# An attention and feed-forward block in two phases on one core: one item of each kind per group of heads, and the layernorms' normalisations moved from ScalarE to VectorE

## What is computed

```python
x = L0_attn_hidden_states                        # 16 x 512 x 512, float32
x = x + _layernorm(attention(_layernorm(x)))     # 32 heads of 16 channels, causal
x = x + _layernorm(ffn(_layernorm(x)))           # 512 -> 1408 -> 512, silu(g) * u
...
q, k, v = split_heads(x @ Wq.T + bq), split_heads(x @ Wk.T + bk), split_heads(x @ Wv.T + bv)
q, k = apply_rope(apply_rope(q, freqs_abs), freqs_temp), apply_rope(apply_rope(k, freqs_abs), freqs_temp)
scores = where(causal, q @ k.T / sqrt(16), -inf)
out = softmax(scores) @ v
return out @ Wo.T + bo
```

## Time and profile before

| what | value |
|---|---|
| median of 3 runs | 2912.18 us (2911.25 to 2916.76) |
| the profiled execution, its own time | 2921.86 us |
| its span, first to last instruction | 2920.1 us |
| mean granted TensorE clock | 0.967 of full speed |
| busy share of the span: PE, DVE, ACT, POOL | 87%, 74%, 48%, 35% |
| attention phase | the start to about 1900 us, 16 sequences |
| feed-forward phase | from about 1900 us to the end |

### The profile page before, as it was taken

The page is one execution under the profiler, slowest core; times in us unless marked ns, Lnnn a source line. Parts: engine busy times, 40 slices in busy tenths (PEclk is TensorE's granted clock), DMA queues, the critical chain, the costliest instruction groups (busy, mean ns, idle before and its releaser), DMA issues. The chain is left out here.

```text
span 2920.1 us, 56573 instructions
## 1 busy us (share of the span) xinstructions
PE 2550.0 (87%) x19584; PEld 1224.1 (42%) x19584; DVE 2174.2 (74%) x6399; ACT 1408.2 (48%) x1838; POOL 1024.1 (35%) x1083
## 2 busy tenths in 40 slices
PE   4888888888888888888888888519999999999997
PEld 1344443443443443443444444204444444444443
DVE  5898998998898888989889888264545554555554
ACT  2566666666666666666666666342222222222221
POOL 4456465465365465564564663200000000000000
PEclk8999999999999999999999999759999999999999
DMA  4232332332332332332322322130111111111111
GB/s 166 78 86 82 93 111 78 104 106 72 115 106 67 106 108 78 108 100 77 108 89 86 114 68 78 47 163 15 72 43 57 43 66 48 53 48 58 57 43 44
DMA packets 125299, 236.54 MB, mean 81 GB/s; under 512 B 11440, under 2 KB 94896, under 8 KB 111920
## 3 DMA queue, kind: packets, MB, share of 16 engines
q1 hardware_dynamic: 123056, 232.84, 25.3%
q10 hardware_dynamic: 2048, 1.05, 0.1%
HBM read 148.39 MB, written 84.41 MB: 80 GB/s over the span
## 5 line engine op out<-in xcount | busy, mean ns | idle before, releaser
L710 DVE CUSTOM_DVE_ANT_0 mx<-mx,causal 128x512 f32<-128x512 f32 (+3 forms) x2048 | 944.2, 519 | 90.0 <-PE mx L831 89.7
L550 ACT ACTIVATE probs<-ts,exp_scale 128x1024 f32<-128x1024 f32 x640 | 711.6, 1112 | 523.4 <-PE ts L845 454.4
L459 POOL TENSOR_SCALAR_AFFINE_SELECT probs<-probs 128x512 f32<-128x512 f32 x512 | 323.3, 648 | 623.1 <-ACT probs L550 623.1
L1255 DVE SCALAR_TENSOR_TENSOR hidden<-gu,up_scale,silu 128x512 f32<-128x512 f32 x176 | 132.0, 750 | 418.1 <-PE gu L1305 418.1
L1114 ACT ACTIVATE silu<-gu,gate_scale 128x512 f32<-128x512 f32 x176 | 120.9, 687 | 631.8 <-PE gu L1305 631.8
L1089 POOL TENSOR_TENSOR f_rstd<-f_var,f_neg_half 128x4 f32<-128x4 f32 x32 | 32.3, 1009 | 929.2 <-DVE f_var L1232 647.3
L1303 PE MATMUL gu<-f_xT_hi,gate_hi 128*128 128x512 f16 x704 | 267.9, 381 | 52.1 <-issue 52.1
L859 PE MATMUL xb<-probs,vs 128*32 128x512 f32 (+3 forms) x4096 | 311.9, 446 | 1.3 <-POOL probs L459 1.0
L710 DVE DVE_READ_ACCUMULATOR2_ANT row_max<- 128x1 f32 x2048 | 288.8, 141 | 0.0
L817 PE MATMUL xb<-xT_hi,w_hi 128*128 128x512 f16 x512 | 204.1, 399 | 85.6 <-DVE aT_lo L681 59.1
L845 PE MATMUL ts<-qT,kT 64*128 64x512 f16 (+3 forms) x2048 | 247.6, 300 | 34.9 <-ACT probs L550 34.7
(11 more groups left out here) (148 smaller groups left out, 4588.9 us busy)
## 6 DMA issues: line engine op xcount, KB each, us to landing
slots<-half SPq DMA_DIRECT2D x260, 128.0 KB, 12.4
qT<-slots SPq DMA_DIRECT2D x128, 256.0 KB, 3.8
kT<-slots SPq DMA_DIRECT2D x128, 256.0 KB, 4.0
xn<-x SPq DMA_DIRECT2D x16, 1024.0 KB, 5.1
xr<-x SPq DMA_DIRECT2D x16, 1024.0 KB, 5.3
slots<-half SPq DMA_DIRECT2D x256, 64.0 KB
x<-xr SPq DMA_DIRECT2D x16, 1024.0 KB, 5.7
f_xn<-x SPq DMA_DIRECT2D x16, 1024.0 KB, 4.8
```

Source lines behind the costliest of these rows:

```text
L459: nc.gpsimd.affine_select(out=d, in_=d, compare_op=ALU.is_ge, fill=0.0, base=0, pattern=[[0, HG], [1, P]], channel_multiplier=-1).then_inc ...
L550: nc.scalar.activation(probs[:, g % 2, u, :, :], ts[:, :, :], ACT.Exp, scale=exp_scale[:, 0:1]).then_inc(ts_read, 1)
L710: last = nc.vector.tensor_tensor_reduce(out=scores, in0=scores, in1=causal[:, T - P * (qt + 1):T], scale=1.0, scalar=-3e38, op0=ALU.add, o ...
```

## The change

The tables of units are replaced by a regular pattern. Each group has one q or k item (units 0 and 1), one transposed tile of x or of the attention result (unit 2), and one v or output item (units 3 and 4). The steps of a q or k item stand in the same units of every group: bias on ACT, cosine on VectorE and all of POOL's part in unit 2, high half in unit 4, low half in unit 0 of the next group, DMAs in units 1 and 2 of it. `xT_hi` and `xT_lo` become double, `aT_hi` and `aT_lo` get a fifth tile. The eight normalisations of a sequence move to VectorE, `minus_mean` and `offset` go, x is loaded, measured and turned nearly one body earlier, ACT's loop is written out, ACT's shift DMAs stand behind the exponential of unit 2, and POOL's first mask moves from unit 2 to unit 4.

```diff
-        xT_hi = sb("xT_hi", [P, NC, T], F16)
-        aT_hi = sb("aT_hi", [P, NC, T], F16)
+        xT_hi = sb("xT_hi", [P, 2, NC, T], F16)
+        aT_hi = sb("aT_hi", [P, NC + 1, T], F16)
...
-        PROJECTED = ((("q", 3, 0), ("k", 3, 0)), (("v", 3, 0), ("out", 0, -1)), (("out", 1, -1), ("out", 2, -1)),
-                     (("q", 0, 1), ("k", 0, 1)), (("out", 3, -1), ("q", 1, 1)), (("k", 1, 1), ("q", 2, 1)),
-                     (("k", 2, 1), ("v", 0, 1)), (("v", 1, 1), ("v", 2, 1)))
-        TRANSPOSED_AT = {4: ("a", 3, -1), 9: ("x", 0, 1), 10: ("x", 1, 1), 14: ("x", 2, 1), 15: ("x", 3, 1),
-                         24: ("a", 0, 0), 29: ("a", 1, 0), 39: ("a", 2, 0)}
-        STATISTICS_AT = {0: 0, 1: 1, 2: 2, 3: 3}
-        VARIANCE_AT = 4
-        NORMALISE_AT = {6: (0, 1), 7: (2,), 8: (3,)}
-        STATISTICS1_AT = {11: 0, 13: 1, 16: 2, 23: 3}
-        VARIANCE1_AT = 24
-        NORMALISE1_AT = {26: (0, 1), 27: (2,), 28: (3,)}
-        RESIDUAL_AT = {27: (0, 1), 28: (2,), 29: (3,)}
...
+        QUERIES_KEYS = [((g - 2) % NG, (g - 2) // NG + 1) for g in range(NG)]
+        V_OR_OUT = (("v", 3, 0), ("out", 0, -1), ("out", 1, -1), ("out", 2, -1), ("out", 3, -1),
+                    ("v", 0, 1), ("v", 1, 1), ("v", 2, 1))
+        TURNED = (("x", 3, 1), ("a", 3, -1), ("x", 0, 2), ("a", 0, 0), ("x", 1, 2), ("a", 1, 0), ("x", 2, 2), ("a", 2, 0))
+        STATISTICS_AT = {5: (0, 1), 6: (2, 3)}
+        VARIANCE_AT = 6
+        ROOT_AT = 8
+        NORMALISE_AT = {10: (0, 1), 11: (2, 3)}
+        STATISTICS1_AT = {11: 0, 16: 1, 21: 2, 26: 3}
+        VARIANCE1_AT = 26
+        ROOT1_AT = 28
+        NORMALISE1_AT = {30: (0, 1), 31: (2, 3)}
+        RESIDUAL_AT = {31: (0, 1), 35: (2, 3)}
...
@@ sync
-                    if s == 16 and exists(i + 1) and (not isinstance(i, int) or i + 2 < NB):
+                    if u == 1 and exists(i + owner):
+                        send_slots(i + owner, n)
+                    if u == 2 and exists(i + owner):
+                        fetch_slots(i + owner, n)
+                    if s == 3 and exists(i + 2):
                         sp.wait_ge(xT_full, NC * (i + 2))
                         sp.dma_start(xn[:, :, :], x[i + 2, :, :, :]).then_inc(x_in, 16)
-                    if s == 31 and exists(i - 1):
+                    if s == 38 and exists(i - 1):
                         sp.wait_ge(x1_ready, NT * i)
                         sp.dma_start(x1[i - 1, :, :, :], xr[:, :, :]).then_inc(x1_out, 16)
-                    if s == 33 and exists(i - 1) and exists(i):
+                    if s == 39 and exists(i - 1) and exists(i):
...
@@ scalar
-            def normalise_x(i, t):
-                if t == 0:
-                    act.wait_ge(offset_ready, i + 1)
-                nc.scalar.activation(xn[:, t, :], xn[:, t, :], ACT.Identity, bias=offset[:, t:t + 1],
-                                     scale=rstd[:, t:t + 1]).then_inc(xn_ready, 1)
...
+                    if u == 2:
+                        if exists(i + owner):
+                            add_bias(i + owner, n)
+                        if exists(i + (g + 1) // NG):
+                            read_shift(i + (g + 1) // NG, (g + 1) % NG)
+                    if u == 3:
+                        kind, c, of = TURNED[g]
+                        if in_turn(kind, i + of):
+                            (high_of_x if kind == "x" else high_of_attention)(i + of, c, bank_of(kind, c))
+                        if exists(i + (g - 1) // NG):
+                            read_weighed(i + (g - 1) // NG, (g - 1) % NG)
                     if exists(i):
                         exponential(i, g, u)
+                    if u == 2 and exists(i + (g + 1) // NG):
                         place_shift(i + (g + 1) // NG, (g + 1) % NG)
...
@@ vector
-                nc.vector.tensor_scalar(minus_mean[:, :], mv[:, :, 0], -1.0, None, ALU.mult)
...
+            def normalise_x(i, t):
+                if t == 0:
+                    dve.wait_ge(rstd_ready, i + 1)
+                nc.vector.tensor_scalar(xn[:, t, :], xn[:, t, :], mv[:, t, 0:1], rstd[:, t:t + 1],
+                                        ALU.subtract, ALU.mult).then_inc(xn_ready, 1)
+
+            def normalise_projected(i, t):
+                if t == 0:
+                    dve.wait_ge(rstd1_ready, i + 1)
+                nc.vector.tensor_scalar(y[:, t, :], y[:, t, :], mv1[:, t, 0:1], rstd1[:, t:t + 1],
+                                        ALU.subtract, ALU.mult).then_inc(projected_normed, 1)
...
@@ tensor
+                    n, owner = QUERIES_KEYS[g]
+                    if u < 2 and exists(i + owner):
+                        project_queries_keys(i, n, owner, u)
...
+                    if u == 2:
+                        kind, c, owner = TURNED[g]
+                        if in_turn(kind, i + owner):
+                            wait_for_bank(pe, i, kind, c)
+                            (turn_x if kind == "x" else turn_attention)(i + owner, c, bank_of(kind, c))
...
+                    if u >= 3:
+                        kind, n, owner = V_OR_OUT[g]
+                        if exists(i + owner):
+                            (project_v if kind == "v" else project_out)(i, n, owner, u - 3)
```

## The result

The changed kernel takes 2930.22 us (median of 20 runs, 2922.33 to 2936.29) against 2914.05 us before (20 runs): a ratio of 1.0051, 95% interval 1.0041 to 1.006. It is slower by half a per cent, where 1.8% less was forecast. The profiled execution has a span of 2928.9 us, against 2920.1 before.

What follows compares the result with a forecast made beforehand. VectorE and PE, neither full, hold each other up. 101.6 + 1.8 + 3.2 + 1.4 + 0.7 + 0.3 = 109.0 us a sequence against 112.8, so 53 us off: 2859 us, range 2824 to 2894 (8 in 10: 2800 to 2930).

Steps and rivals of the forecast that it cites:

- the late load of x: In group 1, x lands late and VectorE waits 1.5 us: +1.8 us a sequence, bounds 0 to +5.
- the statistics of x: In group 1, four statistics and the variance take 3.0 us on VectorE, of which up to 1.9 are free.
- group 6: Four normalisations with no transposition waiting, POOL's residual ahead of its products: +0.7 us a sequence, bounds 0 to 3.
- The mechanism of the old order: Work comes in lumps that stop one engine, then starve the other; PE waits 6.6 us a sequence for low halves.
- The term of 12.7 us for a regular group: On PE, 11.95 us of pure work, 0.65 for `oT` and 0.1 for the bank; eight groups make 101.6.
- the 0.65 us for `oT`: In a regular group PE waits 0.65 us for `oT`, as ScalarE's shift DMAs ahead of it take 1.4 us.
- Group 2, +3.2 and +1.4 us: PE's transposition waits for x's normalisations, +3.2 us (bounds +1.5 to +6); PE's clock then drops, +1.4 (0 to 2).
- Both ends of the attention phase stay: At the attention phase's ends nothing changes: as many q and k items lie before the first scores as before.
- x comes far too late: Rival: SP's queue delays x to 7.6 us into group 1; 114.2 us a sequence, 2932 us, chance 0.10.
- the port decides: Rival: each of eight normalisations waits for a whole POOL instruction; 114.0 us a sequence, 2929 us, chance 0.12.
- the two signs: The forecast is wrong if regular groups take over 13.2 us, or VectorE waits over 4 us for x.

Runs made afterwards that it cites:

- e1: The changed kernel with the load of x moved ahead of the fetch in SyncE's queue: 2870.24 us, ratio 0.9851 to the kernel before.
- e13: e1 with the projected rows' normalisations moved to units 30 and 35, residuals to 31 and 36: 2806.5 us, ratio 0.9636.
- e9: The changed kernel with the early load, normalisations moved to units 9, 10, 30 and 35, residuals to 31 and 36: 2767.34 us, ratio 0.9504.
- e3: The changed kernel with the early load of x and the eight normalisations back on ScalarE: 2794.77 us, ratio 0.9593.
- e6: The kernel before with ScalarE's loop over bodies 1 to 13 written out, nothing else: 2905.88 us, ratio 0.998.
- e10: e3 with the four statistics of x spread over units 5, 6, 7, 8 and the variance in 8: 2772.34 us, ratio 0.9533.
- e11: The changed kernel with the late load kept and only the places of normalisations and residuals changed as in e9: 2826.13 us, ratio 0.9712.
- e4: The kernel before with the eight normalisations on VectorE in the same units, nothing else moved: 2912.24 us, ratio 0.9998.

## Why the prediction was wrong, step by step

Three terms of the sum failed: the late load of x (1.8 us a sequence, measured 4.7), the statistics of x (nearly nothing, measured up to 3.4) and group 6 (0.7, measured 4.7). The bullets take them in turn.

Mean times, from the starts of `weigh`, over twelve whole sequences of each run. Groups 1 and 2 are the time from group 1's `weigh` to group 3's, group 6 from its `weigh` to group 7's; all in us:

| run | groups 1 and 2 | group 6 | sequence |
|---|---|---|---|
| changed kernel | 36.8 | 17.0 | 115.4 |
| e1, early load | 32.1 | 16.8 | 110.4 |
| e13, and the projected rows' places | 31.1 | 12.7 | 105.8 |
| e9, and x's places | 28.0 | 12.7 | 102.7 |
| regular groups | 24.6 | 12.3 | |

- **The mechanism of the old order was right.** PE's waits for low halves in regular groups are gone, and the regular order alone (e3) is worth 119 us against the kernel before (some 5 of them may be ScalarE's loop, e6). It was even undersized. One reading of it was wrong: the 6.6 us a sequence were the row of the weight loads (PEld), and the matmuls' own idle time for `aT_lo` in that view was 37.0 us in 8 sequences, 4.6 each:

```profile
PE xb L817 <- DVE aT_lo L681: 37.0, 32, 2.7
```

  The term of 12.7 us for a regular group measured 12.2 to 12.3: the 0.65 us for `oT` didn't come, because ScalarE issues its shift DMAs while the exponential runs.

```profile
1008.09 1.09 ACT L464 ACTIVATE probs<-ts,exp_scale 128x1024 f32<-128x1024 f32 x1
1008.21 1.20 ACTq L476 DMA_DIRECT2D qT<-shift_rows  x2
1009.46 0.60 ACT L443 ACTIVATE aT_hi<-xb 128x512 f16<-128x512 f32 x1 [0.28 <-issue]
```

  I had put the DMAs behind the exponential, 1.4 us later (the earlier trace rows shows them where nothing covers them).
- **Group 1, +1.8 us for the late x, was mis-sized.** Taking the load forward gave 59 to 60 us, 4.2 a sequence (4.7 in groups 1 and 2 of the table), and the wait is 4.3 to 4.5 us instead of 1.5. The parts: x lands after 7.1 us, not 5.5; x1 is written 1.3 us later in group 7 of the body shown than I put it; the groups between are 0.4 us shorter each, so VectorE is there sooner; and the way from that write to the load's issue is 0.8 us shorter (14.6 us, 988.86 to 1003.45, for 15.4). The longer landing comes in a place where a fetch of `kT` has just been issued and the next sends follow; before, SyncE issued nothing for some 10 us ahead of the load and 16 behind it (load at 683.26 us). That this is its reason is likely and not shown. The range "0 to +5" held the term; the value chosen was at the wrong end.
- **Group 1's statistics, put at nearly nothing, cost something too.** I let 1.9 of their 3.0 us vanish in VectorE's idle time. But with x early and no normalisation held (e9), groups 1 and 2 still take 3.4 us more than two regular ones. In the body shown above, PE waits there for the low half that stands behind the statistics on VectorE:

```profile
1025.27 0.39 PE L750 MATMUL xb<-w_hi,aT_hi 128*128 128x512 f16 x1 [2.76 <-DVE aT_lo L601]
```

  No row had this term. e10 shows that the lump is part of it; how much of the 3.4 us it makes stays open.
- **Group 2, +3.2 and +1.4 us, was right in kind.** The pair in unit 11 is held, PE waits 3.04 us for it where I had 3.6, and the clock drops as in the earlier trace rows. The x half of the edit in e9 gave 39 us, 2.8 a sequence, or 3.1 by the table: less than the 4.6 of the sum.
- **Group 6, +0.7 us, is the step whose reasoning failed.** I let VectorE take the port between POOL's instructions at little loss, and argued that no transposition waits for these rows. But all that stands behind them on VectorE is late: the cosine (itself held), then the low half `xT_lo`, for which PE stops for 3.02 us and falls to the lower clock (0.51 granted from 1091 to 1093 us). The group takes 4.7 us more than a regular one, above the bound of 3, and e13 puts 64 us, 4.6 a sequence, on these rows' places.
- **Summed**, 8 x 12.3 + (22.8 + 13.9 - 24.6) + 4.7 is 115.2, where I had 101.6 + 7.4. The bounds I gave (0 to 5, 1.5 to 6, 0 to 2, 0 to 3) reach 16 together, and the measured extra is 16.8; I narrowed them to 2824 to 2894 as if they could not all be high. Group 6 was above its bound, and the statistics had none of their own.
- **"Both ends of the attention phase stay" was wrong too,** and in favour of the change: the start and the last stretch gave back 21 us of the 36 that the twelve sequences cost. By the measured sequence times alone, 3.0 x 14 = 42 us more, the kernel would have taken some 2955 us.
- **The rivals.** "x comes far too late" and "the port decides" were each half of what happened; neither alone would have made it slower (e1 and e11 are both faster than before). The port rival was priced wrongly as VectorE's total work: in e4 nearly as much work and much of the holding are there, and the time stays. That the two rivals named 2932 and 2929 us, within 2 of the result, is luck: they had 114.2 and 114.0 us a sequence, not 115.4, and unchanged ends. Of the two signs that the prediction had named against itself, one came: over 4 us of waiting for x (4.5). The other, regular groups over 13.2 us, didn't. The range's end of 2930 stood a hair below the result.

What the runs do not separate: in e9 a normalisation is no longer held and no longer stands ahead of the cosine. The holding amounts to 4 x (0.934 - 0.539) + 4 x (1.019 - 0.539) = 3.5 us a sequence, and some of it only moves: the cosine's mean rises from 1.277 to 1.381 us in e9. The gain was 103 / 14 = 7.4; the rest I put down to what stood behind them and to PE's clock, which is argued and not measured apart. A place ahead of the cosine with the port free wasn't tried.

## What to carry to other kernels

A regular order takes out many small waits and leaves little to hide a large one. In the old, gappy order (336.17 - 318.80) / 360 x 112.8 = 5.4 us more of VectorE's time a sequence left the kernel's time as it was (e4, which relieves ScalarE too); in the new one the same instructions cost 104 us more in the wrong units than in the better ones (e11). Place work on a shared port by the other engine's timeline, not by its own due date: four numbers in three tables, with the earlier load, turned +0.5% into -5% (e9), and without it into -3% (e11). And where a load is moved forward by a body, follow its queue back to the last thing that must be waited for in it; moving it ahead of one fetch gave 2% (e1).

## What the runs showed of the hardware that was not expected

- A DMA issue of ScalarE overlaps its own running activation (issue at 1008.21, activation 1008.09 to 1009.18); 0.28 us is lost behind it there, where 1.43 is lost when the issue stands between two activations with none running.
- A pair of float32 `tensor_scalar` of 128x512 in SBUF takes 1.00 us where POOL is idle at its start and 2.26 or 2.92 beside POOL's `tensor_tensor` instructions. This is the port told of in the Trainium skill ("SBUF — State Buffer", SBUF: two separate sides); it says that the loser blocks for the whole instruction, and the trace agrees: the held pair ends at 1084.80, 0.29 us behind POOL's instruction of 1083.23, and the cosine at 1086.47, 0.55 behind that of 1084.59. It agrees to 0.2 us: 0.29 and 0.55 are a little less than such instructions take unheld (0.48 in the earlier trace rows, and 0.67).
- The load of x, 1 MB, takes 7.1 us to land (median) where a fetch and sends of the slots are issued around it, and 5.5 in the place it had before, where none are; in e3, ahead of the fetch, it takes 8.7.
